# Loading nine arrays of the feed stage during attention, with a ring of five slots in place of six

## The reference, cut to what matters

```python
def one_query(qs):                                   # one query token at a time
    return -jnp.sum(jnp.abs(qs[:, None, :, :] - k), axis=-1) * scale
a = jax.nn.softmax(jnp.concatenate([a, zeros], 1), axis=1)[:, :t]
o = (einsum('bsdh,bshw->bdhw', a, vf) + einsum('bdsh,bshw->bdhw', a, vb)).sum(axis=2)
y = (o * sigmoid(1.702 * o)) @ fanin_w.T + fanin_b   # h = h + x + y, x the normed h
...
gate_scores = x @ Wg.T + bg                          # x = layernorm(h)
h = h + sum over the two best experts e of p_e * (relu(x @ W1[e].T + b1[e]) @ W2[e].T + b2[e])
```

## Time and profile before

| | us |
|---|---|
| median of 3 runs | 8665.17 (8665.12 to 8666.93) |
| the profiled execution | 8668.67 |
| its span in the trace | 8666.9 |
| PE busy | 8557.8 (99%) |
| ACT busy | 7722.7 (89%) |
| DVE busy | 7229.8 (83%) |
| the end of attention in the trace (last PE work of it) | 8412.5 |

### The profile page before, as it was taken

The page is one execution under the profiler, slowest core; times in us unless marked ns, Lnnn a source line. Parts: engine busy times, 40 slices in busy tenths (PEclk is TensorE's granted clock), DMA queues, the critical chain, the costliest instruction groups (busy, mean ns, idle before and its releaser), DMA issues. The chain is left out here.

```text
span 8666.9 us, 247342 instructions
## 1 busy us (share of the span) xinstructions
PE 8557.8 (99%) x110998; PEld 6988.5 (81%) x110998; DVE 7229.8 (83%) x5701; ACT 7722.7 (89%) x3712; POOL 42.5 (0%) x35
## 2 busy tenths in 40 slices
PE   8899999999999999999999999999999999999999
PEld 3388998889757888998969899897888888888773
DVE  3688888888888888888888888888888888888874
ACT  2699999999999999999999999999999999999976
POOL 0100000000000000000000000000000000000000
PEclk8899999999999999999999999999999999999999
DMA  3200000000000000000000000000000000000000
GB/s 119 90 17 2 17 2 17 2 2 17 2 17 2 17 2 2 17 2 17 2 17 2 2 17 2 17 2 17 2 2 17 2 17 2 17 2 2 2 12 8
DMA packets 135369, 114.17 MB, mean 13 GB/s; under 512 B 111464, under 2 KB 114984, under 8 KB 134040
## 3 DMA queue, kind: packets, MB, share of 16 engines
q1 hardware_dynamic: 121611, 78.50, 3.8%
q10 hardware_dynamic: 12692, 19.51, 0.7%
HBM read 57.75 MB, written 40.22 MB: 11 GB/s over the span
## 5 line engine op out<-in xcount | busy, mean ns | idle before, releaser
L803 PE MATMUL sc<-ring,window 128*32 128x375 f32 x96000 | 7866.6, 479 | 20.0 <-DVE ring L922 18.5
L854 ACT ACTIVATE ring<-qx,xs 128x3000 f32<-128x3000 f32 x2624 | 7176.6, 2791 | 621.4 <-PE sc L803 618.4
L803 PEld LDWEIGHTS sc<-ring,window 128*32 128x32 f32 x96000 | 6300.5, 110 | 1230.3 <-issue 171.0
L922 DVE TENSOR_SCALAR ring<-qx,xs 128x3000 f32<-128x3000 f32 x3376 | 6130.2, 1836 | 1049.2 <-PE sc L803 990.8
L872 DVE COPY sc<-kept 128x750 f32<-128x750 f32 x385 | 361.9, 940 | 70.2 <-ACT ex L839 53.5
L770 PEld LDWEIGHTS acc<-ext,vf 128*32 128x32 f32 x9408 | 367.5, 109 | 33.1 <-issue 4.2
L757 PE MATMUL acc<-ex,vb 128*32 128x375 f32 x3088 | 384.3, 477 | 1.5 <-DVE ex L887 1.5
L770 PE MATMUL acc<-ext,vf 128*32 128x128 f32 (+1 forms) x9408 | 376.3, 270 | 0.3 <-DVE ext L898 0.2
L898 DVE STREAM_TRANSPOSE ext<-ex 128x768 f32<-128x768 f32 x385 | 374.1, 972 | 0.6
L839 ACT ACTIVATE ex<-sc 128x750 f32<-128x750 f32 x385 | 297.7, 773 | 5.6 <-PE sc L803 5.6
L757 PEld LDWEIGHTS acc<-ex,vb 128*32 128x32 f32 x3088 | 209.2, 108 | 42.8 <-issue 6.0
(11 more groups left out here) (161 smaller groups left out, 781.7 us busy)
## 6 DMA issues: line engine op xcount, KB each, us to landing
qx<-scratch_qk SPq DMA_DIRECT2D x60, 375.0 KB
scratch_v<-ext SPq DMA_DIRECT2D x21, 960.0 KB, 6.8
scratch_qk<-qx ACTq DMA_DIRECT2D x32, 375.0 KB, 3.3
vb<-scratch_v SPq DMA_DIRECT2D x120, 92.0 KB
vf<-scratch_v SPq DMA_DIRECT2D x120, 88.0 KB
scratch_v<-ext ACTq DMA_DIRECT2D x4, 960.0 KB, 6.5
xs<-scratch_x SPq DMA_DIRECT2D x15, 187.5 KB
vb<-scratch_v SPq DMA_DIRECT2D x120, 1.8 KB
```

The costliest lines, as they stand in the source:

```text
L803: mm = pe.matmul(bank[32 * j:32 * j + 32, h, 0:HALF], window[:, HALF_NH * g + j, ROWS - 1 - i:3 * ROWS - 1 - i], ring[:, slot, j, h * HALF ...
L854: act.activation(flat(ring[:, (HALF * g + k) % RING, :, :]), flat(qx[g][:, :, :]), ACT.Abs, bias=xs[g][:, 1, k:k + 1], scale=0.5).then_inc ...
L922: vec.tensor_scalar(flat(ring[:, (HALF * g + k) % RING, :, :]), flat(qx[g][:, :, :]), xs[g][:, 0, k:k + 1], xs[g][:, 1, k:k + 1], ALU.max, ...
```

## The change

Nine of the twelve loads of the feed stage are issued by SP during attention, behind the operands of the last pair, with one semaphore; their arrays live for the whole kernel. To make room, `ring` has five slots, and `xt` of the tokens stage is a view of `oacc` without its first 375 columns. In the feed stage the copies into `hsum` are gone: the matmul reads columns 0 and 127 of `avg` directly. The waits on `w_first`, `w_gate` and `w_up` are gone from PE, ACT, DVE and POOL.

```diff
-RING = 6
+RING = 5
...
+class FeedWeights:
+    def __init__(self, ctx, sbuf, semaphore):
+        self.w1t = sbuf(ctx, "w1t", [128, 2 * NE * 128])
...
+        self.loaded = semaphore(ctx, "feed_weights")
+    def load(self, queue, A):
+        queue.dma_start(self.fant[:, :], A["fant"]).then_inc(self.loaded, 16)
+        queue.dma_start(self.avg[:, :], A["avg"]).then_inc(self.loaded, 16)
...
+        queue.dma_start(self.w1t[:, :], A["w1t"]).then_inc(self.loaded, 16)
+        queue.dma_start(self.b1c[:, :], A["b1c"]).then_inc(self.loaded, 16)
...
+        feed = FeedWeights(whole, sbuf, semaphore)
...
-            xt = sbuf(inner, "xt", [128, TC])
+            xt = oacc[:, 1:, :].rearrange("p b l -> p (b l)")
...
                 load(NPAIR - 1, B - 1, 1)
+                feed.load(sp, A)
                 sp.wait_ge(group_done, NPAIR * NG + 1)
                 sp.sem_inc(pair_in[0], 16 * NLOADS)
+                sp.wait_ge(feed.loaded, 16 * 9)
...
-                sp.dma_start(fant[:, :], A["fant"]).then_inc(w_first, 16)
-                sp.dma_start(avg[:, :], A["avg"]).then_inc(w_first, 16)
-                sp.dma_start(fbc[:, :], A["fbc"]).then_inc(w_first, 16)
-                sp.dma_start(ident[:, :], A["ident"]).then_inc(w_gate, 16)
...
-                sp.dma_start(w1t[:, :], A["w1t"]).then_inc(w_up, 16)
-                sp.dma_start(b1c[:, :], A["b1c"]).then_inc(w_up, 16)
                 sp.dma_start(pick32[:, :, :].rearrange("p e m -> p (e m)"), A["pick"]).then_inc(w_down, 16)
...
-                pool.wait_ge(w_first, 48)
-                pool.tensor_copy(hsum[:, 0:1], avg[:, 0:1]).then_inc(eps_set, 1)
-                pool.tensor_copy(hsum[:, 1:2], avg[:, 127:128]).then_inc(eps_set, 1)
...
-                        mm = pe.matmul(py[0:CH, 2 * k:2 * k + 2], sq[:, k * CH:(k + 1) * CH], hsum[:, :], ...)
+                        mm = pe.matmul(py[0:CH, 2 * k:2 * k + 2], sq[:, k * CH:(k + 1) * CH], avg[:, 0:128:127], ...)
...
-                pe.wait_ge(w_first, 48)
-                pe.wait_ge(eps_set, 3)
+                pe.wait_ge(eps_set, 1)
                 fan(0)
                 mean(0)
-                pe.wait_ge(w_gate, 64)
...
-                pe.wait_ge(w_up, 32)
```

More of the change, by code:

```diff
@@ L116, in load_pair @@
                                 scratch_v[bass.ds(row + 32 * (HBLK - 1), LBLK), cols]).then_inc(into, 16)
+class FeedWeights:
+    def __init__(self, ctx, sbuf, semaphore):
+        self.w1t = sbuf(ctx, "w1t", [128, 2 * NE * 128])
+        self.b1c = sbuf(ctx, "b1c", [128, 2 * NE])
+        self.fant = sbuf(ctx, "fant", [128, 128])
+        self.fbc = sbuf(ctx, "fbc", [128, 1])
+        self.avg = sbuf(ctx, "avg_d", [128, 128])
+        self.ident = sbuf(ctx, "ident_d", [128, 128])
+        self.wgt = sbuf(ctx, "wgt", [128, 2 * NE])
+        self.bg = sbuf(ctx, "bg", [CH, NE])
+        self.first_of = sbuf(ctx, "first_of", [CH, NE])
+        self.loaded = semaphore(ctx, "feed_weights")
+    def load(self, queue, A):
+        queue.dma_start(self.fant[:, :], A["fant"]).then_inc(self.loaded, 16)
+        queue.dma_start(self.avg[:, :], A["avg"]).then_inc(self.loaded, 16)
+        queue.dma_start(self.fbc[:, :], A["fbc"]).then_inc(self.loaded, 16)
+        queue.dma_start(self.ident[:, :], A["ident"]).then_inc(self.loaded, 16)
+        queue.dma_start(self.wgt[:, :], A["wgt"]).then_inc(self.loaded, 16)
+        queue.dma_start(self.bg[:, :], A["bg"].partition_broadcast(CH)).then_inc(self.loaded, 16)
+        queue.dma_start(self.first_of[:, :], A["first"].partition_broadcast(CH)).then_inc(self.loaded, 16)
+        queue.dma_start(self.w1t[:, :], A["w1t"]).then_inc(self.loaded, 16)
+        queue.dma_start(self.b1c[:, :], A["b1c"]).then_inc(self.loaded, 16)
 def build(nc, A, out):
@@ L143, in build @@
             phase_tokens(nc, A, sbuf, psum, semaphore, at, hx, oacc, window, select, scratch_x, scratch_qk, scratch_ks, scratch_v)
-            phase_attend(nc, sbuf, psum, semaphore, at, oacc, window, select, scratch_x, scratch_qk, scratch_ks, scratch_v)
-        phase_feed(nc, A, out, sbuf, psum, semaphore, hx, oacc)
+            phase_attend(nc, A, sbuf, psum, semaphore, at, feed, oacc, window, select, scratch_x, scratch_qk, scratch_ks, scratch_v)
+        phase_feed(nc, A, out, sbuf, psum, semaphore, feed, hx, oacc)
 def phase_tokens(nc, A, sbuf, psum, semaphore, at, hx, oacc, window, select, scratch_x, scratch_qk, scratch_ks, scratch_v):
@@ L673, in _, with phase_attend @@
                             u += 1
-def phase_attend(nc, sbuf, psum, semaphore, at, oacc, window, select, scratch_x, scratch_qk, scratch_ks, scratch_v):
+def phase_attend(nc, A, sbuf, psum, semaphore, at, feed, oacc, window, select, scratch_x, scratch_qk, scratch_ks, scratch_v):
     with ExitStack() as ctx:
@@ L949, in _, with phase_feed @@
                 keep(NPAIR, 1, B)
-def phase_feed(nc, A, out, sbuf, psum, semaphore, hx, oacc):
+def phase_feed(nc, A, out, sbuf, psum, semaphore, feed, hx, oacc):
     with ExitStack() as ctx:
+        w1t, b1c, fant, fbc, avg, ident, wgt, bg, first_of = (feed.w1t, feed.b1c, feed.fant, feed.fbc, feed.avg, feed.ident,
+                                                              feed.wgt, feed.bg, feed.first_of)
         h2 = sbuf(ctx, "h2", [128, TC])
@@ L958, in phase_feed @@
         cp = sbuf(ctx, "cp", [128, TC], BF16)
-        w1t = sbuf(ctx, "w1t", [128, 2 * NE * 128])
-        b1c = sbuf(ctx, "b1c", [128, 2 * NE])
         w2t = sbuf(ctx, "w2t", [128, NE, 2, D])
@@ L964, in phase_feed @@
         pick = sbuf(ctx, "pick", [128, NE, 128], BF16)
[L965 to L968, removed]
         eps = sbuf(ctx, "eps_d", [128, 1])
[L970 to L973, removed]
         cen = sbuf(ctx, "cen_d", [128, EC])
@@ L990, in phase_feed @@
         py = psum(ctx, "py_d", [128, 512])
-        w_first = semaphore(ctx, "w_first")
-        w_gate = semaphore(ctx, "w_gate")
-        w_up = semaphore(ctx, "w_up")
         w_down = semaphore(ctx, "w_down")
@@ L1041, in _ @@
             def _(sp):
-                sp.dma_start(fant[:, :], A["fant"]).then_inc(w_first, 16)
-                sp.dma_start(avg[:, :], A["avg"]).then_inc(w_first, 16)
-                sp.dma_start(fbc[:, :], A["fbc"]).then_inc(w_first, 16)
-                sp.dma_start(ident[:, :], A["ident"]).then_inc(w_gate, 16)
-                sp.dma_start(wgt[:, :], A["wgt"]).then_inc(w_gate, 16)
-                sp.dma_start(bg[:, :], A["bg"].partition_broadcast(CH)).then_inc(w_gate, 16)
-                sp.dma_start(first_of[:, :], A["first"].partition_broadcast(CH)).then_inc(w_gate, 16)
-                sp.dma_start(w1t[:, :], A["w1t"]).then_inc(w_up, 16)
-                sp.dma_start(b1c[:, :], A["b1c"]).then_inc(w_up, 16)
                 sp.dma_start(pick32[:, :, :].rearrange("p e m -> p (e m)"), A["pick"]).then_inc(w_down, 16)
@@ L1092, in var @@
                     for k in range(SUB):
-                        mm = pe.matmul(py[0:CH, 2 * k:2 * k + 2], sq[:, k * CH:(k + 1) * CH], hsum[:, :], start=True, stop=True)
+                        mm = pe.matmul(py[0:CH, 2 * k:2 * k + 2], sq[:, k * CH:(k + 1) * CH], avg[:, 0:128:127], start=True, stop=True)
                     mm.then_inc(var_sum, 1)
@@ L1260, in _ @@
                     swish(c)
-                act.wait_ge(eps_set, 3)
+                act.wait_ge(eps_set, 1)
                 square(0)
@@ L1264, in _ @@
                 exps(0)
-                act.wait_ge(w_up, 32)
                 relu(0)
@@ L1389, in _ @@
                 gated(0)
-                vec.wait_ge(w_first, 48)
                 added(0)
@@ L1396, in _ @@
                 normal(0)
-                vec.wait_ge(w_gate, 64)
                 choose(0)
```

## The result

The changed kernel takes 8683.22 us in the median of 16 runs (8677.89 to 8687.33), the kernel before 8665.88 in 16 runs: 17.3 us more, a ratio of 1.0019 with a 95% interval of 1.0012 to 1.0026. The forecast was 8678 (8666 to 8693), +0.15%. It is slower, beyond the interval. With 0.19% by that ratio and 17.3 us by the medians it lies at the very edge of the 0.2%, 17.3 us, that was called no change.

What follows compares the result with a forecast made beforehand. PE's matmuls set attention's pace. The terms 0 + 8.5 + 4.5 - 1.0 = +12.0 us on the 8665.2 median give 8677.2; 1.2 for one more loop seam with a clock fall gives 8678, range 8666 to 8693.

Steps and rivals of the forecast that it cites:

- Part 1: Ring in an ordinary attention tile: five slots never bring PE to a stop, 0 us lost.
- the 1.6 of the prediction: Ordinary tile with five slots: ACT's row 15 is ready 1.6 us before PE comes for it.
- second rival: Attention: PE waits in every tile, 0.3 us each, 110 us in all, 8788; chance 0.05.
- Part 2: Middle seams: late ACT row 6 delays exponential, fill and DVE's first rows; 8 x 1.06 = 8.5 us lost, bounds 0 and 1.27 each.
- 0.07 us in hand: Middle seams: PE takes DVE's second row of the new pair 0.07 us after it is ready, the only room.
- Part 3: Loop seams: same chain with 0.20 us room; five of seven lose 0.91 each, 4.5 us, two with falling clock lose nothing.
- first rival: Loop seams: PE stands longer and its clock falls at all seven, +18 us, 8683; clock band's chance 0.25.
- Part 4: Start of feed: fan(0) waits for gated(0) instead of POOL's copies, 1.0 us won, bounds 0.5 and 2.5.
- Part 5: Nine loads moved into attention and xt inside oacc: no engine waits for them, 0 us.
- the forecast's own: Whole kernel: band of +6 to +17 us for the forecast itself, chance 0.60.
- the one given to the clock: Whole kernel: band of +17 to +26 us for clock falls at loop seams, chance 0.25.

Runs made afterwards that it cites:

- experiment 1: Kernel before with RING = 5 (five ring slots, not six) and nothing else: 8682.48 us against 8666.29, ratio 1.0019.
- experiment 4: Changed kernel, five slots, with ACT's exponential in the short tile behind its row 4, not row 6: 8665.50 us against 8666.29 for the kernel before, ratio 1.0000.
- experiment 5: Kernel before, six slots, with the short tile's exponential behind ACT's row 4: 8666.51 us against 8665.96, ratio 0.9999.
- experiment 2: Kernel before with xt of the tokens stage as a view of oacc and nothing else: 8665.93 us against 8666.29, ratio 0.9999.
- experiment 3: Kernel before, six slots, only fant and fbc loaded in attention, avg first in feed, copies into hsum gone: 8665.86 us against 8666.29, ratio 0.9999.
- experiment 7: Changed kernel, five slots, with the batch loop written out on SP, PE, ACT and DVE: 8659.11 us, ratio 0.9992 (kernel before: 8665.96 us).
- experiment 6: Kernel before, six slots, with the batch loop written out on SP, PE, ACT and DVE: 8640.91 us against 8665.96, ratio 0.9971.
- experiment 8: Changed kernel with the short tile's exponential early and the batch loop written out: 8640.33 us against 8665.96 for the kernel before, ratio 0.9970.

## Why the prediction was right

**Part 1, ordinary tiles at 0: right.** From `back` to `back` a tile of the changed kernel is 21.68 us (4430.97 to 4452.65 in the timeline of PE):

```profile
4430.97 0.99 PE L788 MATMUL acc<-ex,vb 128*32 128x375 f32 x8
...
4452.65 0.98 PE L788 MATMUL acc<-ex,vb 128*32 128x375 f32 x8
```

In the kernel before it is 21.67 (4419.69 to 4441.36). The smallest time between a row's end at its maker and PE's taking it fell from 2.5 to 1.25 us inside a pair; the 1.6 of the prediction was for row 15 of an undisturbed tile, where the median is 1.5. The second rival (waits in every tile) didn't come, though 1.25 us is all that was left of it.

**Part 2, middle seams: the mechanism right, the size 8.5 for 10.3 us.** Experiments 1 and 4 show the chain from both ends. The term was mis-sized in one step. I let ACT's row 6 wait for its own slot, 1.06 us later. But ACT's rows 2, 4 and 6 follow each other without a pause, and row 2 is the one that waits for a slot: in the changed kernel it starts 6.19 us before `back` (3840.69 against 3846.88), in the kernel before 7.40 (3828.62 against 3836.02):

```profile
3828.62 5.49 ACT L854 ACTIVATE ring<-qx,xs 128x3000 f32<-128x3000 f32 x2 [0.84 <-PE sc L803]
```

It is late by 1.21 here and by 1.29 on average over the eight seams, a whole PE row, and rows 4 and 6 only pass that on. Row 6's slot was free at 3845.93 by the working of the prediction (3846.88 - 1.265 + 0.31), 0.15 us before ACT came to it. Nor did PE have 0.07 us in hand: that is the way from DVE to PE, about 0.05 us at these seams in both kernels, and in the kernel before row 1 of a pair already came 1.36 us after row 0 on average, where experiments 4 and 5 have 1.26. The upper bound that I gave, 1.27 us, was the answer: 260.9 - 250.6 = 10.3, 1.29 a seam.

**Part 3, loop seams: 6.2 us for 4.5 and 1.2, but made up otherwise.** Four stretches around loop seams show the lower clock and three don't; before it was two and five. One of each kind in the changed kernel, the second and the third loop seam:

```profile
2317.00:2352.00 35.00, 31.93 (x428) 18.07 (x424) 28.37 (x23) 30.62 (x17) 0.00 (x0) 1.00 0.01 3
3332.00:3367.00 35.00, 32.18 (x414) 17.55 (x409) 27.32 (x24) 29.53 (x16) 0.00 (x0) 0.95 0.01 3
```

Like is to be compared with like. At full clock a loop seam takes 34.9 us on average in the changed kernel and 34.5 before; with a fall of the clock it takes 36.3 and 35.6. So the slot costs 0.45 us at full clock, where the prediction had 0.91, and 0.6 with a fall, where it had 0. With two falls, as before, that makes 3.5 us; two falls more, at 1.3 each, make the other 2.7.

Two steps of this part failed. The first let the whole delay of DVE's row 1 reach PE's later rows. But in the kernel before PE stood behind row 1 as well, at no wait that the profile shows; at the seam of the earlier trace rows the last of row 1's 16 matmuls comes late:

```profile
3340.00 1.77 PE L803 MATMUL sc<-ring,window 128*32 128x375 f32 x17 [0.18 <-issue]
```

From the start of row 1 to that of row 2 it takes 1.6 to 2.0 us at the five seams at full clock before (1.7 to 2.1 with the early exponential of experiment 4), and 1.3 at those of the changed kernel: the delay took the place of a pause that was there anyway. What makes that pause stays open. The second step looked at row 1 alone where the clock falls. But row 0 had been ready only 0.7 to 0.9 us before PE took it there, so a delay of 1.2 to 1.3 reaches PE at row 0 already: PE begins the pair 0.5 to 0.6 us later at either clock. The first rival of the prediction counts this room of 0.68 us, part 3 doesn't.

The first rival is partly true: two falls more, and four also in the trace of experiment 1, though not at the same seams, against 2, 2, 3, 2 and 1 in the traces of before and of experiments 2 to 5. That five slots bring them isn't shown by so few. PE now stands 2.8 to 3.1 us at these seams where it stood 2.1 to 2.5. The Trainium skill (TensorE: Matmul & The Clock Gate, "Why this matters for your kernels") asks for no long idle gaps of PE between bursts of matmuls, lest the clock drop. The length of the pause alone doesn't tell it in these traces: behind one of 2.12 us the clock fell (3333.29 in experiment 2), behind one of 2.90 us it didn't (7411.15 in the changed kernel). Experiment 7 has neither jump nor fall, and there the same places lose 1.25 us each, the full PE row.

**Part 4, the feed stage: 1.9 us for 1.0.** The start is as worked out: the first matmul at 2.8 us behind the barrier and not 3.7 (8435.14 and 8432.36):

```profile
8432.36 0.10 POOL L1075 MEMSET eps_d<- 128x1 f32 x1 [8183.98 <-POOLq L751]
...
8435.14 1.08 PE L1088 MATMUL px_d<-sg,fant 128*128 128x500 f32 x2 [3.67 <-DVE sg L1307]
```

The other 0.9 us is the clock, which my upper bound had and my value left out. In the first 30 us of the stage the mean granted clock is 0.66 in the changed kernel, 0.60 in the kernel before and 0.72 in experiment 3, and the pair of matmuls above takes 1.08 us at full clock where the earlier trace rows have 2.00 at half. The clock isn't bound to the change: the mean of 0.72 stands also in experiments 5 and 6, which have no feed part. Their stage takes 252.3 and 252.2 us, that of experiments 3, 4 and 8, with the feed part and the same 0.72, takes 251.4, 251.3 and 251.0. So at equal clock the feed part is worth 1.0 us, as predicted; at 0.60 the stage takes 253.0 to 253.6 us without it (before, experiments 1 and 2), at 0.66 251.5 and 251.7 with it (experiment 7 and the changed kernel).

**Part 5, moved loads and moved array: 0, right** (experiments 1 and 2; five slots alone lose 16.2 us, all of the change 17.3).

**The sum.** 10.3 + 6.2 - 1.9 = 14.6 us from the parts, for 13.2 forecast (12.0 and 1.2). That they lie so close is partly luck: the middle seams cost 1.8 us more than forecast and the further falls of the clock 1.5 more, the slot at the loop seams cost 1.0 less, and the feed stage gave 0.9 more. The profiled executions differ by 17.2: the rest is the tokens stage, +4.2, less 1.6 us in small pieces of attention. The medians differ by 17.3 with an interval of about 10 to 23, so that the 14.6 and the 17.3 agree; whether 2 or 3 us more belong to the change stays open. By the bands of the prediction +17.3 stands just outside the forecast's own, +6 to +17, and at the start of the one given to the clock. The mechanism was the forecast's all the same: the clock made 2.7 us of it.

## What to carry to other kernels

How many slots a ring needs isn't read from the steady tile, in which this one had room, but at the places where the side work of a tile is pushed together; there one slot fewer cost one step of the bound engine, 1.3 us, each time, and 0.5 to 0.6 us where a jump made that engine stand anyway. Before memory is spent on a slot to hide such a place, look whether the work that the other engine waits for can be put one step earlier in its own queue: here one line gave the slot's 17 us back. And preload by need: two arrays with 516 bytes a partition between them had all the gain of nine in these traces.

## What the runs showed of the hardware that was not expected

The hardware loop over the batches costs more than the change did. A jump taken by PE, ACT and DVE makes a seam 34.8 us long on average in place of 31.3, and writing the loop out gained 25 us in all (8665.96 to 8640.91) for 7 jumps, 3.5 us each; DVE alone stands 2.2 us behind the jump in the earlier trace rows, and PE 2.2 to 2.6 in experiment 5, where its row had long been ready. At each of the 7 jumps, and at no other seam, ACT also loads its table again, as here in the kernel before; no wait of PE for a row of ACT is listed there.

```profile
3329.50 1.28 ACT L847 ACT_TABLE_LOAD   x1
```

Programs eight times as long in the attention stage showed no cost in exchange: what lies between the seams took 7579.8 us written out and 7581.2 in the loop.
